# A causal attention inside a larger kernel: the tiles of queries taken from the largest to the smallest instead of large and small in turn

## What is computed

```python
cq  = rms_norm(x @ w_qa.T)                    # 192 wide
q   = (cq @ w_qb.T) per head                  # 128 plain + 64 rotated columns
ckv = rms_norm((x @ w_kva.T)[:, :64])         # 64 wide, shared by all heads
k_pe = rope((x @ w_kva.T)[:, 64:])            # 64 wide, shared by all heads
k, v = (ckv @ w_kvb.T) per head
scores = q @ k.T / sqrt(192), future keys masked
out = softmax(scores) @ v, all heads side by side, @ w_o.T
```

## Time and profile before

| | us |
|---|---|
| median of 3 runs | 1986.6 (1986.42 to 1988.61) |
| the profiled execution, its own time | 1982.7 |
| its span, first to last instruction | 1981.0 |
| second pass of the loop over heads (428.82 to 735.42) | 306.6 |
| PE busy over the span | 1658.8 (84%) |
| granted clock of PE, mean | 0.936 |

### The profile page before, as it was taken

The page is one execution under the profiler, slowest core; times in us unless marked ns, Lnnn a source line. Parts: engine busy times, 40 slices in busy tenths (PEclk is TensorE's granted clock), DMA queues, the critical chain, the costliest instruction groups (busy, mean ns, idle before and its releaser), DMA issues. The chain is left out here.

```text
span 1981.0 us, 38768 instructions
## 1 busy us (share of the span) xinstructions
PE 1658.8 (84%) x14479; PEld 1340.4 (68%) x14479; DVE 1319.0 (67%) x3002; ACT 984.1 (50%) x1891; POOL 328.9 (17%) x745
## 2 busy tenths in 40 slices
PE   3768898979899979999988899998759999961697
PEld 2557777767777767777767777778537777841486
DVE  4646777757777767777776777777844544569545
ACT  2436666646666655665655665664422322253432
POOL 3311111111111111111111111111300000053401
PEclk9869999989999999999998999998869999965699
DMA  7000000000000000000000000002100000010000
GB/s 210 1 1 1 2 2 2 2 2 2 2 2 2 1 3 2 2 2 1 2 2 2 2 1 1 2 1 66 46 14 1 1 1 1 1 51 0 0 12 32
DMA packets 17098, 23.75 MB, mean 12 GB/s; under 512 B 8556, under 2 KB 14316, under 8 KB 16772
## 3 DMA queue, kind: packets, MB, share of 16 engines
q1 hardware_dynamic: 11588, 14.77, 2.5%
q10 hardware_dynamic: 5312, 6.33, 1.1%
HBM read 19.00 MB, written 2.10 MB: 11 GB/s over the span
## 5 line engine op out<-in xcount | busy, mean ns | idle before, releaser
L623 ACT ACTIVATE pT_hi<-pT 128x512 f16<-128x512 f32 (+3 forms) x640 | 340.6, 532 | 364.4 <-PE pT L568 361.7
L695 DVE TENSOR_TENSOR pT_lo<-pT,pT_hi 128x512 f16<-128x512 f32 (+3 forms) x640 | 386.1, 606 | 106.2 <-ACT pT_hi L623 102.5
L687 DVE TENSOR_REDUCE cmx<-pS 128x1 f32<-128x512 f32 (+3 forms) x580 | 351.4, 619 | 116.0 <-PE pS L559 112.2
L615 ACT ACTIVATE pr<-pS,nmx 128x512 f32<-128x512 f32 (+3 forms) x640 | 397.9, 622 | 34.1 <-issue 18.9
L554 PE MATMUL pS<-lT_hi,qT_hi 128*128 128x512 f32 (+2 forms) x644 | 290.9, 452 | 77.0 <-ACT pr L615 61.0
L568 PE MATMUL pT<-ident,pr 128*128 128x128 f32 x2176 | 349.8, 277 | 0.0
L582 PE MATMUL pO<-c_hi,pT_hi 128*128 128x65 f16 x2176 | 266.4, 194 | 44.9 <-DVE O L702 32.2
L568 PEld LDWEIGHTS pT<-ident,pr 128*128 128x128 f32 x2176 | 262.9, 142 | 31.0 <-issue 1.1
L583 PE MATMUL pO<-c_lo,pT_hi 128*128 128x65 f16 x2176 | 267.2, 193 | 0.0
L584 PE MATMUL pO<-c_hi,pT_lo 128*128 128x65 f16 x2176 | 264.5, 192 | 0.0
L559 PE MATMUL pS<-lT_hi,qT_lo 128*128 128x512 f32 (+2 forms) x644 | 262.1, 407 | 0.0
(11 more groups left out here) (244 smaller groups left out, 2838.2 us busy)
## 6 DMA issues: line engine op xcount, KB each, us to landing
X<-in_x SPq DMA_DIRECT2D x4, 512.0 KB, 6.9
wo<-in_w_o ACTq DMA_DIRECT2D x1, 2048.0 KB, 14.1
out<-X SPq DMA_DIRECT2D x4, 512.0 KB, 2.6
raw<-in_wd SPq DMA_DIRECT2D x8, 224.0 KB, 2.6
raw<-in_wg SPq DMA_DIRECT2D x8, 220.0 KB, 2.7
raw<-in_wu SPq DMA_DIRECT2D x8, 220.0 KB, 2.5
wqn<-in_w_qn ACTq DMA_DIRECT2D x1, 1536.0 KB, 17.3
intg<-in_qg SPq DMA_DIRECT2D x1, 768.0 KB, 4.4
```

Source lines behind the costliest of these rows:

```text
L615: act.activation(pr[:, at % RING, 0:n * P], pS[at % 4][:, 0:n * P], ACT.Exp, bias=nmx[:, p % 4:p % 4 + 1]).then_inc(sem("exped"), 1)
L623: act.activation(pT_hi[:, at % 4, 0:n * P], pT[at % 2][:, 0:n * P], ACT.Copy).then_inc(sem("p_hi"), 1)
L687: ch.inc(dve.tensor_reduce(cmx[:, p % 2, c:c + 1], pS[at % 4][:, 0:n * P], AX.X, ALU.max))
L695: dve.tensor_tensor(pT_lo[:, at % 4, 0:n * P], pT[at % 2][:, 0:n * P], pT_hi[:, at % 4, 0:n * P], ALU.subtract).then_inc(sem("p_lo"), 1)
```

## The change

One line, in the function that holds the loop over heads:

```diff
-                order = [t for k in range(NT // 2) for t in (NT - 1 - k, k)]
+                order = list(range(NT - 1, -1, -1))
```

## The result

The changed kernel is slower, by less than half a per cent. Over nine runs each, its median is 1992.6 us (1988.8 to 1996.7) against 1985.2 for the kernel before (1982.4 to 1988.6); the ratio is 1.0036, with an interval of 1.0025 to 1.0047. The medians are 7.4 us apart. I had forecast a rise of 9.2 us to 1995.8, in a range of 1983 to 2010.

What follows compares the result with a forecast made beforehand. PE bounds the loop, leaving its waits: -5.9 + 4.7 + 0.2 + 2.1 = +1.1 us idle a pass, +4.4; clock +4.8. 1982.7 becomes 1991.9, plus 3.9 for the median: 1995.8 us, range 1983 to 2010.

Steps and rivals of the forecast that it cites:

- two terms of my sum: Whole loop over heads: PE idle time +1.1 us a pass, and slower clock +1.2 us a pass.
- Sixteen waits of 0.1 us: Tiles 0 to 3, upper bound: each of 16 steps waits 0.1 us more for DVE; loss given as 6.5 us.
- Large groups, -5.9 us: Tiles 14 to 8: first and second heads idle like third heads beside like neighbours; idle 13.1 to 7.2 us a pass.
- The rival in which the large groups keep waiting: Tiles 14 to 8 keep 13.1 us idle, waits coming from each head's own chain; 2014.6 us, chance 0.07.
- Small groups, +4.7 us: Tiles 0 to 3: less PE work covers POOL's chain and DVE; idle 3.7 to 8.4 us a pass.
- 0.4 for fourth heads: Tiles 0 to 3: DVE gets a division in each step, put at 0.1 us for each fourth head.
- Middle groups, +0.2 us: Tiles 4 to 7: tile 4 has fewer blocks to cover with; loss 0.2 us a pass, between -0.5 and +1.
- End of the pass, +2.1 us: Last head: two leftover values steps of two heads wait for divisions, some 1.0 us apart; loss 2.1 us a pass.
- The clock, one fall of some 3 us a pass: PE, groups of tiles 0 and 1: longer waits drop the clock to half speed once, 1.2 us a pass, +4.8 in all.
- My signal for being wrong: PE busy time per pass rising by more than 4 us, which only a slow clock can do; one of three signs.

Runs made afterwards that it cites:

- e9: The changed kernel with POOL's rotation cut from six instructions to two, the sine part for the queries left out: 1958.5 us, ratio 0.9860 to the kernel before.
- e2: The kernel before with tile order 15, 7, 14, 6, 13, 5, 12, 4, 11 to 8, 3, 2, 1, 0: 1989.7 us, ratio 1.0030.
- second trace of the change: The changed kernel, unaltered, timed again in a second comparison on one chip with follow-up kernels: 1992.3 us, ratio 1.0037 to the kernel before.
- e3b: Second run of the changed kernel with unread constant products on PE ahead of the turns in the groups of tiles 2, 1 and 0: 1987.2 us, ratio 1.0014.
- e4b: Second run of the changed kernel with the project of the queries in a group's third head instead of its fourth: 1965.4 us, ratio 0.9903 to before.

## Why the prediction was right, and where it was not

The sign and the size came out, but the two terms of my sum were both off, in opposite directions: idle time +1.1 us a pass forecast and -1.9 measured in the second pass; clock +1.2 forecast and, by the balance, +2.5 to +4.2. The total was right partly by luck. The two are not independent either: by the lengths of the small groups, falls of the clock hid some 0.9 us of waits a pass, which the forecast of idle time did not allow for.

Of the distance between forecast and median (1995.8 and 1992.6), 1.4 us is the base: the kernel before had 1986.6 as the median of three runs and 1985.2 over nine. Two sums of the forecast do not come out as written. Sixteen waits of 0.1 us on top of the 4.7 us of the small groups make 6.3, not 6.5; and the bounds taken together (0 to 2 falls, small groups 3.4 to 6.5) give 1986 to 2008, not 1989 to 2003. Neither changes the forecast.

- **Large groups, -5.9 us:** right to the tenth. Their third heads still idle 2.05 us:

```profile
sum 39.13, PE 37.08 PEld 30.36 DVE 31.43 ACT 24.99 POOL 0.00; mean PE 5.30 PEld 4.34 DVE 4.49 ACT 3.57 POOL 0.00
```

  The earlier trace rows gives 2.05 as well, and their first two heads have come down to the same. The division's waits there fell from 4.6 to 0.6 us, the exponential's from 5.8 to 4.5. The first two heads idle 4.75 us, where 2 x 2.05 + 0.6 = 4.7 was forecast. The rival in which the large groups keep waiting is out. The stage is nevertheless no shorter (167.6 us, 167.4 in the earlier trace rows): with large neighbours it takes over blocks that small neighbours' heads and the pass's end had before. Only idle time summed over the pass shows the gain.
- **Small groups, +4.7 us:** the mechanism was right and the term too large; it measured +3.4. The turns were forecast to wait 1.1, 1.5, 1.8 and 1.9 us and waited 0.72, 1.34, 1.77 and 1.99. Why tile 3 came out 0.34 us better I did not trace. The waits for the division grew from 0.7 to 1.2 us, not to 1.8, and of the 0.4 for fourth heads 0.1 showed. A long wait for POOL seems to give DVE time to catch up: in e9, without it, PE waits 1.9 us for the division in these groups.
- **Middle groups, +0.2 us:** wrong in sign, -1.1, and outside its bounds. Before, values steps in the groups of tiles 5 and 6, between large ones, waited 0.98 and 1.13 us for a half of the transposed probabilities (L623); with like neighbours that is gone, and the waits for exponentials and divisions grew by only 0.9 together. I had not split the 7.3 us of the earlier trace rows by what ended them, and e2 shows the same blind spot: there these groups fell to 5.0.
- **End of the pass, +2.1 us:** +1.7. The values steps are 1.03 and 1.02 us apart, 1.0 was forecast. The waits for divisions there grew from 0.8 to 3.1 us; the restart wait happened to be 0.4 shorter.
- **The clock, one fall of some 3 us a pass:** in the small groups of the profiled run this is what happened in passes 2 to 4 (at 718.4, 1025.6 and 1332.8 us, 3.4 us each), with two in the first. The second trace of the change had two in its first and third pass and one in the others. What I left out is the start of the next pass: the half-speed stretch there was 13.6, 10.2 and 17.1 us before (passes 2 to 4), 13.6, 17.1 and 17.1 in the first trace of the change and 20.5, 20.5 and 17.1 in the second. The price of 0.4 us for each at half speed was right for PE's busy time (0.37 over thirty passes), but in the small groups a fall cost only 0.5 to 1.0 us of length. That the clock matters at all is shown by e3b against the change in the same comparison; that the waits for POOL bring it down, by e9 and e4b, in which they are gone or down to 0.9 us and the falls in the small groups are gone. Why a start is longer in one trace than in another is open.
- **My signal for being wrong**, busy time up by more than 4 us a pass, was reached in the first pass (4.25), and by the cause that I had named for it.

The rule of the Trainium skill (Perfetto Trace Analysis, Optimization Strategy) says that interleaving regimes may help where the most-contended engine changes from one to the other. It is no measure of this case, since PE is the busiest engine in the large groups and in the small ones alike.

What the trace says is that a small tile needs a bigger neighbour: 2.8 us of waits for POOL interleaved, 5.8 in a row. For the large tiles interleaving with small and middle ones costs 5.9 us. Once POOL's chain starts early, the interleaved order is the slower one (1970.6 against 1965.4 us), and the best order tried gives small tiles middle neighbours and leaves the large ones alone.

## What to carry to other kernels

When work items of different size share one in-order pipeline, ask for each side chain how long it is (here 4.94 us from project to turn) and what its neighbours put over it: a like neighbour is good for the large items and bad for the small ones, and starting the chain a step earlier is worth more than any order tried with the late start (14 us in the old order, 27 in the new one). Sum idle time over a whole period and not by stage, split it by what ends it, and carry half-speed time as a term of its own beside it; a saving in idle time that leaves one wait of near 2 us among short work can be eaten by the clock.

## What the hardware did that I had not expected

- A single wait of 1.99 us, with PE busy 1.23 of 3.20 us around it, was followed by a fall to 1.2 GHz, where 1.3 us in the earlier trace rows was not. The wait alone does not decide. In the second pass of the second trace the fall came one group earlier, behind a wait of 1.78 us, and the wait of 1.99 us behind it left the clock at 1.00; in the first pass of both traces, and the third of the second, there were two falls, with the same waits. No run here says what decides.
- Short products that compute nothing can pay: 64 a pass in the small groups gave back 5.1 us, and 30 a pass at the start 7.5 us.
- PE's busy time in a pass is not a constant of the program but nearly one of the clock: 271.4 to 278.4 us for the same 2865 products, of which the half-speed time (10.8 to 29.6 us a pass) explains all but 0.6 us (standard deviation; the largest is 1.4).
